# Reordering the side work of the paired MLP stage: when a tile is added and scaled, when the next pair's operands are turned, combined and split, and when the weight combinations are made

## The chip, the cores and the metric

The kernel runs on one core of one Trainium2 chip. The metric is device time in microseconds (us) of one execution; three runs of the kernel before gave 3091.52, 3093.77 and 3094.1 us, median 3093.77. The engines are named as in the profile: PE (TensorE, matrix products), DVE (VectorE), ACT (ScalarE), POOL (GpSimd), and SP, whose queue starts every DMA that is spoken of here.

## The reference, cut to what matters

`x` is 8192 tokens of 512 channels. It is normalised, sent through a state-space layer with an MLP behind it and, beside that, through a gated MLP on 4-bit quantised values; the results are added to `x`.

```
x   = L0_attn_x                                   # (2, 4096, 512)
xn  = layernorm(x)
a   = xn + ssm_scan(rmsnorm(xn, scale1))
h   = rmsnorm(a, scale2)
h   = gelu(h @ w1 + b1) @ w2 + b2                 # 512 -> 2048 -> 512
out = x + (a + h) + fp4_gated_mlp(xn)             # 512 -> 1408 -> 512
```

The change touches only the fourth and fifth line: the two products with `w1` and `w2` and what prepares their input.

## The kernel before, in words

The 8192 tokens are 64 tiles of 128. Up to about 1760 us the kernel does the quantised MLP, the convolution form of the scan and the first tiles' preparation. Then two stages follow.

**The block stage (about 1760 to 2099 us).** Sixteen tiles, four blocks of four, go through `mlp1(n)` (12 matmuls, one 128-wide slice of the hidden layer) and `mlp2(n)` (12 matmuls) for n = 0 to 63; PE runs `mlp1(n)`, `mlp2(n-2)`, `mlp1(n+1)`, and so on. Each float32 product is made as three products of a high and a low part. Between them, at fixed n, the other engines do side work. `mlp_steps` lists where the tiles of the next block are added (`tile_add`), scaled (`tile_root`) and split (`tile_low`, `tile_high`). `early_steps` lists the same for the first eight tiles of the next stage, at n = 44 to 57. `combine_steps` lists where 16 pieces of `w1` are combined for the next stage: ACT scales (`combine_scale`), POOL makes four sums (`combine_sums`, L2222 to L2227), ACT takes the high part (L1995), POOL the low part (`combine_low`, L2233, `wl`), and SP stores both.

**The paired stage (2099 to 3092 us).** Six pairs of blocks, 8 tiles (1024 tokens) each. `unit(c, u)`, u = 0 to 7, makes the first product by a seven-product scheme (`product`, L1203, 42 matmuls: k = 0 to 6) whose results DVE adds up (L1671, L1676, L1682, L1692, L1696) and ACT sends through gelu. `rest(c)` finishes the second product (`second(c, i, j)`, L1225, 12 matmuls for each i from 14 to 31). PE's order is fixed: in the rest it does i = 14, 15, 16, ... without anything between. For each i DVE copies the high part of the gelu's result (`second_part`, L1660, the CAST rows) and POOL subtracts to get the low part (`second_rest`, L2249). The buffers G, G2x hold three such i, so DVE may copy i when PE has finished i - 3, and PE needs copy and low part when it comes to i.

Side work in a unit, for the next pair's tile `o`: SP loads it, DVE does `tile_add` (L1542, L1546), ACT squares it, POOL adds bias and residual (`tile_z`, L2208, L2213), DVE does `tile_root` (L1552, ten instructions on one column, then L1558 over the tile), SP stores the sum (`store_sum`, L718) and the scaled tile (`store_normed`, L722, to `r_N`).

Side work in a rest, for the next pair: its tiles come back from `r_N` in four quarters (`quarters(c, i)`, L741, eight DMAs with 128-byte pieces). Quarter 1 overwrites the buffers of tile 7, so it waits until that tile's `store_normed` has landed (`d_ho`). Then for each quarter DVE transposes twice (`conv_turn`, L1612), makes four half-size sums in PSUM (`conv_sums`, L1628, L1629, L1631, L1633), ACT takes high parts (`conv_high`), DVE and POOL take low parts (`conv_low`, L1639/L1643 on DVE, L2239/L2242 on POOL). The sums use PSUM banks 0 to 3, which hold the second product's first half until `sum_out` (L1708) has read them. All engines run their queues in program order, so a wait of one instruction holds all behind it.

## Time and profile before

| | |
|---|---|
| median of 3 runs | 3093.77 us |
| the profiled execution, device time | 3093.77 us |
| its span, first to last instruction | 3092.0 us |
| PE busy | 2991.3 us (97%) |
| DVE busy | 2177.3 us (70%) |
| ACT, POOL busy | 1146.4 us (37%), 1519.8 us (49%) |
| mean granted PE clock | 0.998 |

PE is busy nearly all the time; the other engines matter only where they make it wait. The 12 matmuls of one i are issued in 2.72 us (the row of 24 that starts at 2218.18 is followed by the next i at 2223.76). A row's own duration is longer, since matmuls overlap.

### The profile page before, as it was taken

The numbers are of one execution on the slowest core, as the hardware profiler recorded it, in microseconds if no ns is written. First come the engines' busy times: TensorE is split into PE (matmuls) and PEld (weight loads), VectorE is DVE, ScalarE is ACT, GpSimd is POOL, SyncE is SP. The second block draws the span as 40 slices with busy tenths as digits, with TensorE's granted clock in tenths as the row PEclk, the third lists the DMA queues.
The fourth block names the chain that finished last, engine by engine and source line by source line (L and its number), as shares of the span: only waits on it lengthen the run. The fifth ranks groups of instructions, "written<-read, shape, count | busy, mean of one in ns | idle before, by whom it ended". The sixth has DMA issues, their size and how long they took to land.

```text
span 3092.0 us, 43985 instructions
## 1 busy us (share of the span) xinstructions
PE 2991.3 (97%) x14573; PEld 2417.7 (78%) x14573; DVE 2177.3 (70%) x4451; ACT 1146.4 (37%) x1934; POOL 1519.8 (49%) x1417
## 2 busy tenths in 40 slices
PE   5799999999999999999999899999999999999999
PEld 3678888888887777777777788788888888888887
DVE  7798898887877677777777676776665656565622
ACT  5445656644453343433433343222222222222220
POOL 7556666665555555554555235423444434353513
PEclk9999999999999999999999999999999999999999
DMA  4133343346766666666643458777777676768541
GB/s 126 48 86 93 118 118 107 97 133 180 191 175 171 162 168 163 154 162 172 166 120 99 126 134 203 170 178 205 203 179 205 174 214 168 206 165 218 150 127 48
DMA packets 965425, 469.89 MB, mean 152 GB/s; under 512 B 688080, under 2 KB 816336, under 8 KB 962640
## 3 DMA queue, kind: packets, MB, share of 16 engines
q1 hardware_dynamic: 965200, 467.08, 58.0%
q8 instruction: 118, 1.93, 0.3%
q14 instruction: 107, 0.88, 0.1%
HBM read 330.06 MB, written 136.87 MB: 151 GB/s over the span
## 4 chain that ended last, share of the span: by engine, by line
PE 66%; DVE 18%; issue 5%; POOL 5%; DMA 2%; ACT 2%; SPq 1%; DVEq 0%; POOLq 0%; ACTq 0%
PE bank L1225 16%; PE bank L1203 15%; PE bank L1029 14%; PE bank L1051 7%; PE bank L1152 4%; PE bank L1168 4%; DVE qs L1349 3%; POOL qa L2124 2%; DVE qa L1366 2%; PE bank L1092 2%; DVE qs L1360 2%; DVE qa L1322 2%; POOL qa L2118 1%; DVE qb L1374 1%; PE bank L999 1%
## 5 line engine op out<-in xcount | busy, mean ns | idle before, releaser
L1029 PE MATMUL bank<-XT,Wu 128*128 128x512 f32 (+1 forms) x2148 | 515.5, 389 | 16.1 <-DVE sg L1314 15.8
L1029 PE MATMUL bank<-XT,Wg 128*128 128x512 f32 (+1 forms) x2148 | 522.8, 392 | 7.3 <-DVE Wd L1381 7.3
L1051 PE MATMUL bank<-Wd,HT 128*128 128x512 f32 x2112 | 515.5, 393 | 6.6 <-POOL HT L2132 5.3
L1029 PEld LDWEIGHTS bank<-XT,Wu 128*128 128x128 f32 x2148 | 400.9, 190 | 106.7 <-issue 25.9
L2124 POOL TENSOR_TENSOR qa<-qb,qs 128x512 f32<-128x512 f32 (+2 forms) x277 | 308.5, 1114 | 342.3 <-DVE qb L1374 337.8
L1051 PEld LDWEIGHTS bank<-Wd,HT 128*128 128x128 f32 x2112 | 391.8, 188 | 106.2 <-issue 15.4
L1029 PEld LDWEIGHTS bank<-XT,Wg 128*128 128x128 f32 x2148 | 397.4, 189 | 95.9 <-DVE Wd L1381 9.4
L1225 PE MATMUL bank<-Wp,G 128*128 128x512 f32 x1536 | 388.4, 389 | 5.1 <-POOL G L2249 5.1
L1203 PE MATMUL bank<-HC,Wp 128*128 128x512 f32 x1440 | 361.7, 389 | 1.7 <-POOL WH L2242 1.7
L2132 POOL TENSOR_TENSOR HT<-qb,HT 128x512 fp32r<-128x512 f32 (+1 forms) x179 | 229.9, 1284 | 242.2 <-ACT HT L1817 242.0
L1225 PEld LDWEIGHTS bank<-Wp,G 128*128 128x128 f32 x1536 | 288.1, 188 | 66.1 <-POOL G L2249 6.3
L2118 POOL TENSOR_TENSOR qa<-qa,qs 128x512 f32<-128x512 f32 (+1 forms) x243 | 263.0, 1082 | 109.1 <-DVE qs L1354 109.1
L1203 PEld LDWEIGHTS bank<-HC,Wp 128*128 128x128 f32 x1440 | 270.2, 188 | 58.2 <-POOL WH L2242 2.1
L1817 ACT ACTIVATE HT<-qb 128x512 fp32r<-128x512 f32 (+1 forms) x179 | 112.2, 627 | 414.1 <-DVE qb L1328 414.0
L1366 DVE SCALAR_TENSOR_TENSOR qa<-qb,qa 128x512 f32<-128x512 f32 (+2 forms) x149 | 120.8, 811 | 140.7 <-ACT qb L1789 140.5
L2249 POOL TENSOR_TENSOR G<-gf,G 128x512 fp32r<-128x512 f32 x64 | 83.4, 1304 | 254.9 <-DVE G L1660 254.9
L1225 PE MATMUL bank<-Wp,G2x 128*128 128x512 f32 x768 | 198.1, 389 | 3.4 <-POOL G2x L2249 3.4
L1152 PE MATMUL bank<-hT,Wp 128*128 128x512 f32 x768 | 188.3, 395 | 8.1 <-DVE Wp L1537 5.4
L1168 PE MATMUL bank<-Wp,G 128*128 128x512 f32 x768 | 184.7, 390 | 4.4 <-DVE G L1588 3.2
L1824 ACT ACTIVATE sg<-bank 128x512 f32<-128x512 f32 (+1 forms) x179 | 105.5, 590 | 203.7 <-PE bank L1029 200.3
L1152 PEld LDWEIGHTS bank<-hT,Wp 128*128 128x128 f32 x768 | 146.4, 191 | 39.5 <-issue 5.8
L1168 PEld LDWEIGHTS bank<-Wp,G 128*128 128x128 f32 x768 | 144.0, 188 | 36.0 <-DVE G L1588 6.0
(199 smaller groups left out, 4543.4 us busy)
## 6 DMA issues: line engine op xcount, KB each, us to landing
Wp<-r_A SPq DMA_DIRECT2D x336, 256.0 KB, 3.5
px<-in_L_attn_x_dram SPq DMA_DIRECT2D x128, 256.0 KB, 3.3
xin<-in_L_attn_x_dram SPq DMA_DIRECT2D x128, 256.0 KB, 3.4
sT<-r_K SPq DMA_DIRECT2D x128, 256.0 KB, 4.2
r_Z<-xin SPq DMA_DIRECT2D x64, 256.0 KB, 2.4
r_U<-ub SPq DMA_DIRECT2D x16, 1024.0 KB, 6.7
sU<-r_U SPq DMA_DIRECT2D x32, 512.0 KB, 5.1
r_Y<-sY SPq DMA_DIRECT2D x16, 1024.0 KB, 5.6
```

The source lines that it names most:

```text
L1029: ins = e.matmul(bk[:, 0:n], W[wh][:, k, :], inputs(xh, w, k), start=(k == 0 and p_ == 0), stop=(k == KD - 1 and p_ == 2))
L1051: ins = e.matmul(DNB[t % 4][:], HT[hh][:, w % 2, a * P:(a + 1) * P], Wd[wh][:, f, :], start=(w == first(n) and p_ == 0), stop=(w == last(n ...
L1152: ins = e.matmul(bk[:], Wp[f][wh][:, 0, k * P:(k + 1) * P], hT[xh][b % 2][:, k, :], start=(k == 0 and p_ == 0), stop=(k == KD - 1 and p_ = ...
L1168: ins = e.matmul(ACC[j][:], G2[gh][:, n % 2, j * P:(j + 1) * P], Wp[f][wh][:, 1, :], start=(f == 0 and p_ == 0), stop=(f == 15 and p_ == 2))
L1203: ins = e.matmul(bank[bk][:], ring(q)[:, 256 * wh_ + P * kt:256 * wh_ + P * kt + P], combined(b, xh)[:, kt], start=(k in OPENS and kt == 0 ...
L1225: ins = e.matmul(bank[4 * half + j][:], (second_high(q), second_low(q))[gh][:, j * P:(j + 1) * P], Wp[f][wh_][:, 1, :], start=(f == 0 and ...
L1366: e.scalar_tensor_tensor(Aa, Bb, FLOOR, Aa, ALU.max, ALU.add).then_inc(s_t, 1)
L1817: e.activation(HT[0][:, w % 2, 0:n], qb[:, m % 2, 0:n], ACT.Copy).then_inc(s_hh, 1)
L1824: e.activation(sg[:, 0:n], GB[:, 0:n], ACT.Silu).then_inc(s_sg, 1)
L2118: e.tensor_tensor(blk(qa[:, m % 4, 0:n]), blk(job_in(m)), bc(qs[:, m % 4, 1, 0:n // 16], n // 16), ALU.mult).then_inc(s_pa, 1)
L2124: e.tensor_tensor(blk(qa[:, m % 4, 0:n]), blk(qb[:, m % 2, 0:n]), bc(qs[:, m % 4, 0, 0:n // 16], n // 16), ALU.mult).then_inc(s_ph, 1)
L2132: e.tensor_tensor(lo, qb[:, m % 2, 0:n], hi.bitcast(F32), ALU.subtract).then_inc(s_hl, 1)
```

## The change

Five things move; no instruction's work is changed.

1. `combine_steps`: the 16 combinations stand at n = 18, 20, ..., 48 instead of 12, 14, ..., 42.
2. In a unit, `tile_add` stands before the copy `second_part(c, 2u)` and L1682 (behind them before); `tile_root` stands before L1696 (behind it before); on ACT `tile_square` moves ahead of a gelu; on SP `store_sum` moves from k = 5 to k = 4.
3. In a rest, DVE's `conv_turn` stands at i = 17, 18, 24, 26 (before: 17, 21, 26, 29), `conv_sums` at 20, 21, 25, 28 (20, 23, 27, 30), `conv_low` at 22, 23, 27, 29 (22, 25, 28, 31), and the first four `sum_out` all at i = 19 (two at 19, two at 21). POOL's `conv_low` stands at 17, 20, 25, 27 (18, 22, 27, 30).
4. ACT's `conv_high` takes the first two parts of quarters 0 and 1 first; `high_done` counts accordingly.
5. SP issues `quarters(c+1, 2)` behind the loads of residuals 4 to 7.

```diff
 def combine_steps(n):
-    return [k for k in range(16) if 12 + 2 * k == n]
+    return [k for k in range(16) if 18 + 2 * k == n]
...
 sync: unit
-                    if k == 5 and more:
+                    if k == 4 and more:
                         store_sum(o)
 sync: rest
                 for i in range(4):
                     tile_result(c, i)
-                if more:
-                    quarters(c + 1, 2)
                 for i in range(4, 8):
                     residual_in(c, i)
                 if more:
+                    quarters(c + 1, 2)
                     quarters(c + 1, 3)
 vector: unit
                 e.tensor_tensor(u3[:], bank[6][:], u2[:], ALU.add).then_inc(s_add, 1)
+                if c + 1 < PAIRS:
+                    tile_add(o)
                 second_part(c, 2 * u if u < 7 else 14)
...
-                if c + 1 < PAIRS:
-                    tile_add(o)
...
                 e.tensor_tensor(gelued(0, 2 * u + 1), bank[6][:], u2[:], ALU.add).then_inc(s_add, 1)
+                if c + 1 < PAIRS:
+                    tile_root(o)
...
                 e.tensor_tensor(gelued(1, 2 * u), bank[7][:], u2[:], ALU.add).then_inc(s_add, 1)
-                if c + 1 < PAIRS:
-                    tile_root(o)
                 if u == 7:
                     second_part(c, 15)
 vector: rest
-                    if i in (19, 21):
-                        sum_out(c, i - 19)
-                        sum_out(c, i - 18)
-                    if i in (17, 21, 26, 29) and more:
-                        conv_turn(d, (17, 21, 26, 29).index(i))
...
+                    if i in (17, 18, 24, 26) and more:
+                        conv_turn(d, (17, 18, 24, 26).index(i))
+                    if i == 19:
+                        for j in range(4):
+                            sum_out(c, j)
...
```

**Place one: DVE, the end of a pair's unit 7** (first pair). L1682, L1692, L1696 add up products 4, 5 and 6; L1542 and L1546 are `tile_add`; L1552 to L1558 are `tile_root`; the last CAST is the copy for i = 15. Before:

```order
L1676 TENSOR_TENSOR u<-bank,u 128x512
L1660 CAST G2x<-GX 128x512
L1682 TENSOR_TENSOR G<-bank,u 128x512
L1542 TENSOR_SCALAR xl<-xl,mv,rst 128x512
L1546 TENSOR_TENSOR xl<-xl,yl 128x512
L1692 TENSOR_TENSOR gf<-bank,u 128x512
L1696 TENSOR_TENSOR G<-bank,u 128x512
L1552 TENSOR_SCALAR rs<-rs 128x1
...
L1558 TENSOR_SCALAR xl<-xl,rs 128x512
L1660 CAST G<-GX 128x512
```

The same place in the changed kernel, whose line numbers are 3 to 5 higher (L1695 is L1692, L1555 is L1552, L1561 is L1558, L1701 is L1696, L1663 is L1660):

```order
L1549 TENSOR_TENSOR xl<-xl,yl 128x512
L1663 CAST G2x<-GX 128x512
L1687 TENSOR_TENSOR G<-bank,u 128x512
L1695 TENSOR_TENSOR gf<-bank,u 128x512
L1555 TENSOR_SCALAR rs<-rs 128x1
...
L1561 TENSOR_SCALAR xl<-xl,rs 128x512
L1701 TENSOR_TENSOR G<-bank,u 128x512
L1663 CAST G<-GX 128x512
```

The scaling now lies between the additions of products 5 and 6, and the copy for i = 15 follows the last addition directly.

**Place two: DVE, the rest, i = 17 to 21.** L1612 are the transposes of `conv_turn`, the L1660 rows the copies, L1708 `sum_out`, L1628 to L1633 `conv_sums`. Before, from the transposes of quarter 0:

```order
L1612 STREAM_TRANSPOSE xl<-yl 128x512
L1660 CAST G<-GX 128x512 x2
L1708 TENSOR_TENSOR zq<-bank,zq 128x512 x2
L1660 CAST G2x<-GX 128x512
L1628 TENSOR_TENSOR bank<-xl,st 128x256
L1629 TENSOR_TENSOR bank<-xl 128x256
L1631 TENSOR_TENSOR bank<-xl,bank 128x256
L1633 TENSOR_TENSOR bank<-st,bank 128x256
L1660 CAST G<-GX 128x512
L1708 TENSOR_TENSOR gf<-bank,gf 128x512 x2
L1612 STREAM_TRANSPOSE yl<-xl 128x512
L1612 STREAM_TRANSPOSE xl<-yl 128x512
```

In the changed kernel (L1615 transposes, L1663 copies, L1711 `sum_out`, L1631 to L1636 `conv_sums`), the copy for i = 18 is the first CAST:

```order
L1663 CAST G<-GX 128x512
L1615 STREAM_TRANSPOSE yl<-xl 128x512
L1615 STREAM_TRANSPOSE xl<-yl 128x512
L1663 CAST G<-GX 128x512
L1711 TENSOR_TENSOR zq<-bank,zq 128x512 x2
L1711 TENSOR_TENSOR gf<-bank,gf 128x512 x2
L1663 CAST G2x<-GX 128x512
L1631 TENSOR_TENSOR bank<-xl,st 128x256
L1632 TENSOR_TENSOR bank<-xl 128x256
L1634 TENSOR_TENSOR bank<-xl,bank 128x256
L1636 TENSOR_TENSOR bank<-st,bank 128x256
L1663 CAST G<-GX 128x512
```

The transposes of quarter 1 moved ahead of the copy for i = 19, the four `sum_out` ahead of the copy for i = 20.

**Place three: POOL, the end of the combinations in the block stage.** L2222 to L2227 are the sums, L2233 is `combine_low`, L2208 and L2213 are `tile_z`. Before:

```order
L2222 TENSOR_TENSOR wt<-wt 128x128
L2223 TENSOR_TENSOR wt<-wt 128x128
L2225 TENSOR_TENSOR wt<-wt 128x128
L2227 TENSOR_TENSOR wt<-wt 128x128
L2233 TENSOR_TENSOR wl<-wt,wh 128x1024
L2208 TENSOR_TENSOR zl<-zl,b2r 128x512
L2213 TENSOR_TENSOR yl<-zl,xl 128x512
```

In the changed kernel (L2225 to L2230 the sums, L2236 `combine_low`, L2211 and L2216 `tile_z`):

```order
L2211 TENSOR_TENSOR zl<-zl,b2r 128x512
L2216 TENSOR_TENSOR yl<-zl,xl 128x512
L2225 TENSOR_TENSOR wt<-wt 128x128
L2226 TENSOR_TENSOR wt<-wt 128x128
L2228 TENSOR_TENSOR wt<-wt 128x128
L2230 TENSOR_TENSOR wt<-wt 128x128
L2236 TENSOR_TENSOR wl<-wt,wh 128x1024
L2211 TENSOR_TENSOR zl<-zl,b2r 128x512
```

The first row that writes `zl` is the first of the next stage's tiles: before, all combinations lay ahead of these tiles; now the last three lie among them.

## Rows read from the trace of the kernel before

**Rows 1.** PE's waits, paired stage: engine line <- releaser: us, times, longest.

```profile
PE bank L1225 <- POOL G L2249: 5.1, 3, 1.7
PE bank L1225 <- POOL G2x L2249: 3.4, 2, 1.7
```

**Rows 2.** PE's waits from 1820 to 2025 us, block stage.

```profile
PE bank L1168 <- DVE G L1588: 3.2, 2, 1.8
...
PE bank L1168 <- DVE zx L1599: 1.2, 2, 0.7
```

**Rows 3.** Timeline of PE, first rest: start us, us, what, [idle before <- releaser].

```profile
2213.61 2.88 PE L1225 MATMUL bank<-Wp,G2x 128*128 128x512 f32 x12
2218.18 5.74 PE L1225 MATMUL bank<-Wp,G 128*128 128x512 f32 x24 [1.69 <-POOL G L2249]
2223.76 2.88 PE L1225 MATMUL bank<-Wp,G2x 128*128 128x512 f32 x12
```

**Rows 4.** Timeline of DVE and POOL, end of unit 7.

```profile
2211.09 0.69 DVE L1692 TENSOR_TENSOR gf<-bank,u 128x512 f32<-128x512 f32 x1 [0.17 <-PE bank L1203]
2213.13 0.69 DVE L1696 TENSOR_TENSOR G<-bank,u 128x512 f32<-128x512 f32 x1 [1.35 <-PE bank L1203]
...
2213.74 0.14 DVE L1552 TENSOR_SCALAR rs<-rs 128x1 f32<-128x1 f32 x1
...
2216.26 0.42 DVE L1660 CAST G<-GX 128x512 fp32r<-128x512 f32 x1
...
2216.76 1.38 POOL L2249 TENSOR_TENSOR G<-GX,G 128x512 fp32r<-128x512 f32 x1 [3.60 <-DVE G L1660]
2216.93 1.48 DVE L1660 CAST G2x<-gf 128x512 fp32r<-128x512 f32 x1
```

**Rows 5.** Timeline of SP's queue, first rest, and one row of the third.

```profile
2216.37 0.32 SPq L722 DMA_DIRECT2D r_N<-xl  x1
...
2218.81 2.60 SPq L741 DMA_DIRECT2D xl<-r_N  x4
2221.46 2.67 SPq L741 DMA_DIRECT2D yl<-r_N  x4
...
2546.75 0.32 SPq L722 DMA_DIRECT2D r_N<-xl  x1
2550.28 1.24 SPq L741 DMA_DIRECT2D xl<-r_N  x2
```

**Rows 6.** DMA issues, 2210 to 2218.5 us, then 2218.5 to 2224.5: median us to landing.

```profile
Wp<-r_A SPq DMA_DIRECT2D x4, 256.0 KB, 4.7
...
r_N<-xl SPq DMA_DIRECT2D x1, 256.0 KB, 2.3
...
yl<-r_N SPq DMA_DIRECT2D x4, 64.0 KB, 2.4
```

**Rows 7.** Timeline of DVE and POOL, first rest, i = 20 to 23.

```profile
2226.75 0.43 DVE L1660 CAST G2x<-GX 128x512 fp32r<-128x512 f32 x1 [0.74 <-PE bank L1225]
...
2229.65 0.42 DVE L1660 CAST G<-GX 128x512 fp32r<-128x512 f32 x1
...
2229.99 1.28 DVE L1708 TENSOR_TENSOR gf<-bank,gf 128x512 f32<-128x512 f32 x2
...
2231.18 0.70 DVE L1612 STREAM_TRANSPOSE yl<-xl 128x512 f32<-128x512 f32 x1
...
2232.56 0.38 DVE L1660 CAST G<-GX 128x512 fp32r<-128x512 f32 x1
...
2234.27 1.29 POOL L2239 TENSOR_TENSOR HC<-yl,HC 128x512 fp32r<-128x512 f32 x1
...
2235.52 0.92 POOL L2242 TENSOR_TENSOR WH<-xl,WH 128x256 fp32r<-128x256 f32 x1
```

**Rows 8.** Timeline of POOL and DVE around n = 44.

```profile
1981.57 2.50 POOL L2233 TENSOR_TENSOR wl<-wt,wh 128x1024 fp32r<-128x1024 f32 x1 [1.17 <-ACT wh L1995]
1981.88 2.73 DVE L1588 TENSOR_TENSOR G<-gf,G 128x512 fp32r<-128x512 f32 x1
```

More of the change, by code:

```diff
@@ L482, in high_done @@
         def high_done(c, i, x):
-            return 20 * c + 5 * i + x + 1
+            order = [(a, b) for a in range(4) for b in range(5)]
+            if c:
+                order = ([(a, b) for a in (0, 1) for b in (0, 1)] + [(a, b) for a in (0, 1) for b in (2, 3, 4)]
+                         + order[10:])
+            return 20 * c + order.index((i, x)) + 1
         def combined(m, h):
@@ L1714, in rest @@
                     second_part(c, i)
-                    if i in (19, 21):
-                        sum_out(c, i - 19)
-                        sum_out(c, i - 18)
-                    if i in (17, 21, 26, 29) and more:
-                        conv_turn(d, (17, 21, 26, 29).index(i))
-                    if i in (20, 23, 27, 30) and more:
-                        conv_sums(d, (20, 23, 27, 30).index(i))
-                    if i in (22, 25, 28, 31) and more:
-                        conv_low(d, (22, 25, 28, 31).index(i))
+                    if i in (17, 18, 24, 26) and more:
[3 more added lines that the diff above has]
+                            sum_out(c, j)
+                    if i in (20, 21, 25, 28) and more:
+                        conv_sums(d, (20, 21, 25, 28).index(i))
+                    if i in (22, 23, 27, 29) and more:
+                        conv_low(d, (22, 23, 27, 29).index(i))
                 for j in range(4, 8):
@@ L2043, in unit @@
                 e.activation(gelued(0, 2 * u), bank[4][:], ACT.Gelu, bias=vec[:, 2 * u:2 * u + 1]).then_inc(s_gc, 1)
+                if c + 1 < PAIRS:
+                    tile_square(OLD + 8 * (c + 1) + u)
                 for n, (half, f) in enumerate(((1, 2 * u + 1), (0, 2 * u + 1), (1, 2 * u))):
@@ L2046, in unit @@
                     e.activation(gelued(half, f), gelued(half, f), ACT.Gelu, bias=vec[:, f:f + 1]).then_inc(s_gc, 1)
-                    if n == 0 and c + 1 < PAIRS:
-                        tile_square(OLD + 8 * (c + 1) + u)
             def rest(c):
                 if c + 1 < PAIRS:
-                    for i in range(4):
-                        for x in range(5):
-                            conv_high(c + 1, i, x)
+                    for i, x in ([(a, b) for a in (0, 1) for b in (0, 1)] + [(a, b) for a in (0, 1) for b in (2, 3, 4)]
+                                 + [(a, b) for a in (2, 3) for b in range(5)]):
+                        conv_high(c + 1, i, x)
             for m in range(NJ + 4):
@@ L2263, in rest @@
                     second_rest(c, i)
-                    if i in (18, 22, 27, 30) and c + 1 < PAIRS:
-                        conv_low(c + 1, (18, 22, 27, 30).index(i))
+                    if i in (17, 20, 25, 27) and c + 1 < PAIRS:
+                        conv_low(c + 1, (17, 20, 25, 27).index(i))
             for m in range(NJ + 3):
```

## The prediction

> **What bounds the kernel now.** I read the busy shares first (PE 97%), then PE's waits by stage, because with PE this full only its waits can be won. From its start at 2099 us the paired stage has 8.5 us of waits for the low part that POOL makes, five of them [rows 1]; from 1820 to 2025 us PE waits 4.4 us for DVE [rows 2]. The earlier stages are not touched. Parts one to three speak of the five waits; of the rest only half of the 1.2 us for L1599 lies where the change frees anything. So all that can be won is some 10 us, 0.3% of 3092.
>
> The five waits are one wait five times. In the timeline of the first rest PE starts i = 14 at 2213.61. Twelve matmuls take 2.72 us (24 of them end with the next start: (2223.76 - 2218.18) / 2 = 2.79, of which 0.07 is a slower re-entry), so i = 15 could start at 2216.33; it starts at 2218.18, 1.85 us late [rows 3]. DVE's timeline says why: L1696 starts at 2213.13, the scaling of the tile fills 2213.74 to 2216.26, only then comes the copy for i = 15, POOL's low part follows at 2216.76, and PE goes 1.92 us after the copy's start [rows 4]. All that follows is arithmetic on this ledger; every time is of the first rest.
>
> **Part one, the scaling moved ahead of L1696.** L1692 starts at 2211.09 and its successor 0.61 us later, as L1696's does [rows 4]. The scaling takes 2216.26 - 2213.74 = 2.52 us, so L1696 starts at 2211.70 + 2.52 = 2214.22, the copy at 2214.83, and PE at 2214.83 + 1.92 = 2216.75. The wait shrinks from 1.85 to 0.42 us: 1.43 us won, 7.2 us in five rests. POOL is idle there before the copy (3.60 us in its row), so nothing lengthens the scaling. L1696 is 1.1 us later; what waits for it is the fourth bank of i = 14 at 2213.61 + 2.04 = 2215.65, after its end at 2214.91. In units 0 to 6 its readers are the next unit's fifth product, several us away: nothing. `tile_add` now starts after L1676, some 5 us earlier than before; its load is issued a unit ahead: nothing. The sooner store of the sum and the moved square cost nothing either: PE waits for neither, and both only come before the scaling that needs them.
>
> **Part two, the transposes of quarter 1 at i = 18.** This is the step that can take the gain back. DVE now waits, with the copy for i = 19 behind it, until quarter 1 has landed. Before, they stood at 2231.18 [rows 7], long after. Quarter 1 starts when the scaled tile 7 has landed in `r_N`: stored at 2216.37, first quarter DMA at 2218.81, the eighth 4.7 us later, and landed 2.4 us after that: 2225.9 [rows 5, 6]. In the third rest the same step took 3.53 us instead of 2.44 [rows 5]; the five are 2.44, 3.24, 3.53, 3.46 and 2.66 us, mean 3.07. These differences are not the store's own time: it took 2.3 us to land in the first rest, when the four ring loads issued just before it took 4.7 [rows 6], so the queue was still draining loads. In the changed kernel the store is issued at 2214.33, 2.04 us earlier, but behind the same loads. At best all 2.04 us are won, at worst none, as the loads decide. I take 1.2: SP gets to quarter 0 and the loads behind it about 1 us sooner, since tile 6 too is stored sooner. Then quarter 1 has landed, on the average of five rests, at 2225.9 + 0.63 - 1.2 = 2225.3.
>
> The Trainium skill, "DMA: Bandwidth & Descriptors", section on queues, rings and completion order, says that each of the 16 DMA engines takes a ring's descriptors in order, while completion of whole DMAs is not in order of issue. By it the store stays behind the loads. The 4.7 and 2.3 us agree with a queue that drains; no run here shows one DMA engine by itself.
>
> From the landing the ledger goes on. Two transposes and the step to the copy take 2232.56 - 2231.18 = 1.38 us [rows 7]: the copy for i = 19 starts at 2226.7, PE can start i = 19 at 2228.6. PE wants it at 2216.75 + 4 x 2.72 + 0.1 = 2227.7. A new wait of 0.9 us. (With the landing at 2223.9 it would be none; at 2226.5, 2.1.)
>
> **Part three, what follows at i = 19 to 22.** Four `sum_out` in a row, at (2231.18 - 2229.99) / 2 = 0.60 us each [rows 7], behind 0.34 us for the copy, put the copy for i = 20 at 2229.5: PE could have it at 2231.4, wants it at 2231.3, no wait worth counting. POOL then does the low part of 20 and the two low parts of quarter 1, which stood at i = 22: 1.29 + 0.92 us [rows 7], and only then that of 21. That ends 0.5 + 1.3 + 2.2 + 1.3 = 5.3 us after the copy for 20, at 2234.8; PE wants i = 21 at 2234.1: 0.7 us. DVE's second `conv_sums` takes 2.9 us like the first (2229.65 - 2226.75) [rows 7], and leaves i = 22 late by 0.1 to 0.2. From i = 23 DVE is ahead again: quarters 2 and 3 land about 5 us before PE needs what is made of them. The conversions end earlier than before, but PE has no wait at a next pair's start that could go (the five of [rows 1] are all in the rests), so that wins nothing.
>
> Sum of a rest: 0.42 + 0.9 + 0.7 + 0.15 and 0.07 to 0.1 us of re-entry at each of three: 2.4 us, against 1.85 + 0.11 before: +0.4 us, five times: +2 us. Bounds: quarter 1 early and no collision, 5 x (0.42 - 1.96) = -7.7 us; landings as before, 5 x (3.7 - 1.96) = +8.7 us.
>
> A rule speaks against part three. The Trainium skill, "SBUF — State Buffer", section on the shared port pair, says that GpSimd and a VectorE copy (or an operation with two SBUF inputs) lock each other out for a whole instruction. The trace agrees: a copy of 0.42 us took 1.48 where a POOL operation of 1.38 us had started before it [rows 4]. The 2.9 us of `conv_sums` hold one such stop; by the rule the second one, now beside POOL's extra pair, could hold a second of 1.3 us.
>
> **Part four, the combinations 6 steps later.** At n = 18 to 42 the same work stands as before, so I leave those waits as they are. At 12 to 17 POOL and ACT are freed; the only wait near is half of the 1.2 us for L1599 [rows 2]: at most 0.6 us won. At 43 to 49 three combinations join the additions and scalings of four tiles. What such a meeting costs is in the rows: L1588 took 2.73 us instead of 0.69 beside L2233's 2.50 [rows 8], and PE's two waits for L1588 are 3.2 us [rows 2]. L1599 at n = 49, for which PE waits 0.7 us already [rows 2], gets the last combination just before it. Bounds -0.6 and +6 us (three meetings of 2 us); I take +1.5, one such wait (1.6), as DVE runs ahead of PE in most of that stretch.
>
> **Sum.** The profiled execution took 3093.8 us, which is also the median (span 3092.0). 3093.8 + 2 + 1.5 = 3097.3, so 3097 us. This kernel's measurement tells 0.2%, 6 us, from no change.
>
> **Rivals.**
> - *The waits simply go* (faster). Quarter 1 lands by 2223.9, POOL and DVE don't collide, and part four is neutral: 3093.8 - 7.7 = 3086 us. For it: the store is issued 2.04 us sooner, SP is less behind. Against: the quarter-1 step took up to 3.53 us before, in a queue full of loads.
> - *The landing decides* (slower). The ring loads hold the store, quarter 1 lands when it did, DVE stands at i = 18 with the copy for 19 behind it: +8.7, with part four +10: 3104 us. It decides from a landing 0.6 us later than I take. For it: in four of five rests the wait for the landing was over 2.6 us.
> - *The combinations among the early tiles* (slower). Rest as forecast, three meetings instead of one: +2 + 6 = 3102 us. Against it: no wait at 44 to 48 now, so there is slack to eat first.
>
> **How the numbers follow.** My forecast, within 0.2% (3087.6 to 3100): 0.45. The waits simply go: 0.22. The landing decides 0.23, the combinations 0.10: slower 0.33. The likeliest is the forecast, 3097 us. The range: 3086 holds nearly all of the faster case, whose end is about the most that can be won; 3107 covers both slower cases and part of their sum. So 3086 to 3107; the forecast's own range is 3089 to 3100.
>
> **What would show it.** Part one: the rests' wait at i = 15 at 0.4 us, the copy for i = 15 right behind the last addition. Part two: DVE idle before the third transpose, released by a DMA, and PE waiting for POOL's low part at i = 19. Part three: PE waiting at i = 21, POOL's `conv_low` pair just before. Part four: new waits of PE for L1588's successor between 1987 and 2020 us and a longer one for L1599's. It would be wrong if the rests have no wait at all, if the scaling between the additions made a unit's product wait, or if waits appear at i = 24 or later.

## The result and the profile after

| | before | changed |
|---|---|---|
| median (4 runs each, same chip) | 3093.93 us | 3112.88 us |
| lowest to highest | 3091.52 to 3094.47 | 3110.65 to 3115.39 |
| ratio, with 95% interval | | 1.0062 [1.005, 1.0075] |
| the profiled execution, device time | 3093.77 us | 3109.46 us |
| its span | 3092.0 us | 3107.7 us |

The changed kernel is slower by 19 us. The forecast was 3097 us with a range of 3086 to 3107, so the time lies 6 us beyond the upper end, and it isn't within 0.2% of the kernel before either. Over all 21 executions on record the changed kernel took 3109.46 to 3116.33 us. The profiled one is the lowest of them, 3.4 us below the median of the four, so its trace accounts for 15.7 us of the 19. One execution of the kernel before, beside the first four experiments, took 6119.76 us at a mean granted clock of 0.543; no comparison uses it.

The page of the changed kernel, busy time and share of the span by engine, then PE's waits in the paired stage (from 2098 us; engine, line, releaser: us in total, times, longest):

```profile
PE 2998.3 (96%) x14573; PEld 2417.2 (78%) x14573; DVE 2148.6 (69%) x4451; ACT 1142.6 (37%) x1934; POOL 1519.4 (49%) x1417
```

```profile
PE bank L1228 <- POOL G L2252: 8.3, 10, 2.4
PE bank L1228 <- POOL G2x L2252: 3.5, 5, 1.5
PE bank L1206 <- DVE GX L1687: 2.6, 1, 2.6
PE bank L1206 <- POOL WH L2245: 1.8, 1, 1.8
```

The five waits for the low part [rows 1] have become fifteen, 11.8 us where 8.5 stood, and there is a sixteenth for DVE, which did not exist. PE's busy time rose by 7 us with the same 14573 matmuls, for two reasons. After a wait the next two matmuls come later than the idle time says (at i = 15 it is 0.27 us of idleness, a start 0.43 us late and another 0.11 us for the matmul behind it), so each new wait costs about 0.27 us more than it shows; and some matmuls ran at the lower clock, of which more below.

By stage, from the starts of PE's matmuls: up to n = 2 of the block stage -1.0 us (1735.2 before, 1734.2 after; over all kernels profiled here this point lies between 1734.0 and 1736.1, so that is scatter), from there to the first matmul of the paired stage 370.5 instead of 364.0 us, and the paired stage 1002.9 instead of 992.7 us. So two places lost 6.5 and 10.2 us.

**The paired stage.** Timeline of the first rest in the changed kernel, PE, DVE, POOL and SP's queue put together (start us, us, what, [idle before <- releaser]):

```profile
2221.97 2.88 PE L1228 MATMUL bank<-Wp,G2x 128*128 128x512 f32 x12
2222.57 0.68 DVE L1701 TENSOR_TENSOR G<-bank,u 128x512 f32<-128x512 f32 x1
2222.68 0.32 SPq L726 DMA_DIRECT2D r_N<-xl  x1
2223.17 0.42 DVE L1663 CAST G<-GX 128x512 fp32r<-128x512 f32 x1
2225.12 5.73 PE L1228 MATMUL bank<-Wp,G 128*128 128x512 f32 x24 [0.27 <-POOL G L2252]
2226.87 2.60 SPq L745 DMA_DIRECT2D xl<-r_N  x4
2229.51 2.67 SPq L745 DMA_DIRECT2D yl<-r_N  x4
2235.52 0.71 DVE L1615 STREAM_TRANSPOSE yl<-xl 128x512 f32<-128x512 f32 x1 [6.21 <-DMA yl<-r_N]
2236.91 0.38 DVE L1663 CAST G<-GX 128x512 fp32r<-128x512 f32 x1
2238.69 3.06 PE L1228 MATMUL bank<-Wp,G 128*128 128x512 f32 x12 [2.40 <-POOL G L2252]
...
2241.46 1.48 POOL L2242 TENSOR_TENSOR HC<-yl,HC 128x512 fp32r<-128x512 f32 x1
2242.90 0.92 POOL L2245 TENSOR_TENSOR WH<-xl,WH 128x256 fp32r<-128x256 f32 x1
2245.29 5.82 PE L1228 MATMUL bank<-Wp,G 128*128 128x512 f32 x24 [0.72 <-POOL G L2252]
```

This is the ledger of the forecast with real numbers in it. The copy for i = 15 follows the last addition at once (L1701 2222.57, CAST 2223.17) and PE starts i = 15 at 2225.12, 0.43 us late instead of 1.85 [rows 3]. Then DVE stands for 6.21 us in front of quarter 1; the copy for i = 19 comes at 2236.91 and PE sits idle for 2.4 us there. At i = 21 POOL has the pair L2242, L2245 ahead of PE's low part, and PE is 0.9 us late. ("Late" is the matmul's start against the 227 ns at which matmuls follow each other; it is 0.16 us more than the idle time in brackets.) Over the five rests i = 15 is late by 0.43 to 0.44 us; i = 19 by 2.56, 0.77, 1.69, 0.72 and 1.97 (mean 1.54); i = 21 by 0.87 to 0.90.

The landing that sets i = 19 came, counted from the start of i = 14, after 13.53, 11.77, 12.66, 11.67 and 12.99 us, mean 12.5; before it was 12.32 to 13.47, mean 13.0. The store of tile 7 was issued 2.05 us sooner. The DMA issues of the changed kernel around it (2221 to 2226.5 us) tell where that went; the last number is the median us to landing:

```profile
Wp<-r_A SPq DMA_DIRECT2D x1, 256.0 KB, 4.6
r_N<-xl SPq DMA_DIRECT2D x1, 256.0 KB, 4.0
```

The same store needed 2.3 us to land before [rows 6]. It was issued 2.05 us sooner and took 1.7 us longer. Over the five rests it took 3.7 to 5.0 us (mean 4.3) where it took 2.3 to 3.4 before (mean 2.9), so 0.7 of the 2.05 us were won. In the first rest the last of the eight quarter DMAs also landed 3.95 us after its issue instead of 2.44, so that this landing came 1.2 us later than before, and the mean gain at the landing is 0.44 us. That the loads ahead of the store hold it is what the rows suggest; no run takes the loads away. e10 below moves the same store the other way: issued 1.27 us later, it took 2.0 to 2.7 us (mean 2.2) and landed only 0.5 us later.

The sixteenth wait is in the first unit of the first pair. Timeline of SP's queue, DVE and PE there, changed kernel:

```profile
2107.85 0.34 SPq L699 DMA_DIRECT2D xl<-in_L_attn_x_dram  x1
2108.24 2.54 SPq L705 DMA_DIRECT2D yl<-r_Y  x2
2114.03 0.69 DVE L1549 TENSOR_TENSOR xl<-xl,yl 128x512 f32<-128x512 f32 x1 [2.08 <-DMA yl<-r_Y]
2114.97 0.69 DVE L1687 TENSOR_TENSOR GX<-bank,u 128x512 f32<-128x512 f32 x1
2115.71 1.67 PE L1206 MATMUL bank<-WH,Wp 128*128 128x512 f32 x6 [2.56 <-DVE GX L1687]
```

For every later unit the tile's load is issued a unit ahead. This one is issued in the unit that uses it: `tile_add` now meets it before it has landed, and the addition of product 4 (L1687), for which PE waits, stands behind.

**The block stage.** PE's waits in the changed kernel from 1985 to 2030 us:

```profile
PE bank L1171 <- DVE zx L1602: 5.8, 1, 5.8
PE bank L1155 <- ACT gf L1980: 2.2, 2, 1.9
```

Before, the same window has 0.75 us for L1599, L1602's predecessor, and at its left edge the end of a wait of 1.8 us for L1588 at 1984.7, which the changed kernel has at 1979.0 (1.5 us), outside. The timeline of POOL, DVE and PE in the changed kernel shows how 0.75 became 5.8:

```profile
1993.58 1.99 DVE L1293 SCALAR_TENSOR_TENSOR rs<-rs 128x1 f32<-128x1 f32 x1
...
1998.85 0.63 ACT L1945 ACTIVATE yl<-xl 128x512 f32<-128x512 f32 x1 [6.83 <-DVE xl L1549]
...
2006.16 0.49 DVE L1561 TENSOR_SCALAR xl<-xl,rs 128x512 f32<-128x512 f32 x1
...
2007.09 2.87 POOL L2236 TENSOR_TENSOR wl<-wt,wh 128x1024 fp32r<-128x1024 f32 x1 [1.17 <-ACT wh L1998]
2007.63 2.62 DVE L1545 TENSOR_SCALAR xl<-xl,mv,rst 128x512 f32<-128x512 f32 x1
2010.29 1.66 DVE L1549 TENSOR_TENSOR xl<-xl,yl 128x512 f32<-128x512 f32 x1
...
2017.74 2.34 POOL L2236 TENSOR_TENSOR wl<-wt,wh 128x1024 fp32r<-128x1024 f32 x1 [1.17 <-ACT wh L1998]
2017.79 2.57 DVE L1561 TENSOR_SCALAR xl<-xl,rs 128x512 f32<-128x512 f32 x1
...
2021.34 2.48 DVE L1602 TENSOR_TENSOR zx<-bank,zx 128x512 f32<-128x512 f32 x4
...
2022.17 4.52 PE L1171 MATMUL bank<-Wp,G 128*128 128x512 f32 x12 [5.82 <-DVE zx L1602]
```

The last combinations now lie among `tile_add` and `tile_root` of the next stage's tiles. L1561 takes 0.49 us by itself and 2.57 beside POOL's L2236; L1545 takes 2.62 instead of 0.54; L1549 1.66 instead of 0.69. These three are 2.08 + 2.08 + 0.97 = 5.1 us, and the wait grew by 5.1, but that is not yet the whole account. The same stretch before starts and ends with these rows:

```profile
2002.03 0.43 DVE L1586 CAST G<-gf 128x512 fp32r<-128x512 f32 x1 [1.37 <-ACT gf L1977]
...
2017.54 2.48 DVE L1599 TENSOR_TENSOR zx<-bank,zx 128x512 f32<-128x512 f32 x4
```

From the copy to the result's additions that is 15.51 us; in the changed kernel, from the same copy at 2000.18 to L1602 at 2021.34, it is 21.16, so 5.65 more. The three stops make 5.13 of it, the one-column instructions of the two scalings 1.49, as they now also meet POOL's four sums, and two stops by `tile_z` that stood there before are 0.99 shorter. The idle 1.36 us of DVE ahead of a copy are no slack: ACT's square waits for the `tile_add`, the gelu stands behind the square, and the copy needs the gelu.

The wait of 1.9 us for ACT at 2000.3 comes in the main in the same way, one tile earlier: L1293, on one column, takes 1.99 us instead of 0.16 beside a L2236 of 2.84 us that started at 1992.70, the `tile_add` behind it is late, and ACT's square waits 6.83 us for it. So far this is arithmetic on rows; e9 below shortens such POOL operations and sees what goes. The Trainium skill, "SBUF — State Buffer", section "SBUF: two separate sides", says that a VectorE operation in a mode that uses two ports and a GpSimd operation exclude each other for the whole of one instruction, whichever started first. The trace agrees: POOL's operation ends at 2020.08, and DVE's, which started beside it, 0.28 us later.

And a long wait costs twice. The windows of 2022.0 to 2025.5 us, changed kernel, and of 2022 to 2026 us, before (start:end, us, busy PE (x), PEld (x), DVE (x), ACT (x), POOL (x), granted PE clock, DMA share, GB/s):

```profile
2022.00:2025.50 3.50, 3.33 (x8) 2.68 (x9) 3.47 (x6) 0.00 (x0) 1.28 (x1) 0.51 0.82 177
```

```profile
2022.00:2026.00 4.00, 4.00 (x20) 3.30 (x19) 2.50 (x7) 1.99 (x4) 1.29 (x1) 1.00 0.93 250
```

After the 5.8 us of idleness the granted clock is 0.51, that is 1.2 GHz: 8 matmuls stand 427 ns apart instead of 227. The row of twelve takes 4.52 us instead of 3.01 at the same step before, after a wait of 0.75: 1.5 us more; after the 1.94 us wait at 2000.3 it is 1.4. In sum the stretch from n = 44 to the paired stage lost 7.3 us of waits (5.1 + 1.9 + 0.3) and some 3.5 of clock and slower starts behind the waits, 11 us. That the stage lost only 6.5 comes from an old wait at its start: 5.42 us before a first matmul at 1764.2, followed by matmuls at the lower clock, became 2.99 at full clock. In the profiles of kernels that leave this stage as it was, this wait lies anywhere from 2.9 to 5.4 us, so I don't count it to the change. The wait for L1588 at 1984 us scatters in the same way: 1.8 to 3.6 us in the eight profiles that have the combinations at 12.

### The profile page after: what moved, and what is told of

Same layout as the page of the kernel before. It is cut to its first block, busy times and chain, and to the rows that moved or that the text cites. A ratio compares the mean times of both kernels' runs of the same rounds, so it can differ in the third digit from the quotient of the medians.

```text
span 3107.7 us, 43985 instructions
## 1 busy us (share of the span) xinstructions
PE 2998.3 (96%) x14573; PEld 2417.2 (78%) x14573; DVE 2148.6 (69%) x4451; ACT 1142.6 (37%) x1934; POOL 1519.4 (49%) x1417
## 4 chain that ended last, share of the span: by engine, by line
PE 62%; DVE 18%; issue 6%; POOL 5%; DMA 4%; ACT 2%; SPq 2%; DVEq 0%; ACTq 0%; POOLq 0%
PE bank L1032 14%; PE bank L1206 14%; PE bank L1228 14%; PE bank L1054 7%; PE bank L1155 4%; PE bank L1171 3%; DVE qs L1352 3%; POOL qa L2127 2%; DVE qa L1369 2%; PE bank L1095 2%; DVE qs L1363 2%; DVE qa L1325 2%; POOL qa L2121 1%; DVE qb L1377 1%; PE bank L1002 1%
```

## The experiments

All are edits of the kernel before or of the changed one, 5 to 11 executions each, against the kernel before. Its median was 3094.15 us beside the first four, 3093.96 beside the next four, 3092.88 beside the last four. "Stage" numbers are from the profile of each run: block stage 364.0 and paired stage 992.7 us for the kernel before.

| run | median us | ratio [95%] | block, paired stage |
|---|---|---|---|
| e1_comb18: before, combinations at 18 + 2k | 3101.5 | 1.0027 [1.0017, 1.0038] | 370.5, 992.7 |
| e2_nocomb: changed, combinations back at 12 | 3105.2 | 1.0035 [1.0021, 1.0048] | 364.3, 1005.3 |
| e3_unit: before, only the unit's reordering | 3090.2 | 0.9991 [0.9982, 0.9999] | 365.5, 988.6 |
| e4_rest: before, only the rest's reordering | 3103.15 | 1.0032 [1.002, 1.0045] | 363.6, 1004.0 |
| e5_turn19: e2, quarter 1 turned at i = 19 | 3102.36 | 1.0031 [1.002, 1.0043] | 363.1, 1001.8 |
| e6_turn19_pool22: e5, POOL's pair at i = 22 | 3103.12 | 1.0036 [1.0022, 1.005] | 362.7, 1000.5 |
| e7_comb16: before, combinations at 16 + 2k | 3100.78 | 1.0026 [1.0015, 1.0036] | 372.7, 992.8 |
| e8_comb6: before, combinations at 6 + 2k | 3096.72 | 1.0008 [0.9999, 1.0017] | 366.3, 992.7 |
| e9_comb18_narrow: e1, last low parts short | 3096.28 | 1.0011 [1.0003, 1.002] | 366.7, 992.9 |
| e10_copyfirst: before, copy 15 before the scaling | 3085.76 | 0.9977 [0.9968, 0.9986] | 362.4, 985.6 |
| e11_unit_g0: e3 but for the first unit | 3087.11 | 0.9979 [0.9971, 0.9988] | 363.6, 986.4 |
| e12_copyfirst_comb10: e10, combinations at 10 + 2k | 3087.77 | 0.9985 [0.9976, 0.9994] | 365.2, 985.6 |

The paired stage of the kernel before repeats within 0.3 us (992.7 to 992.9 in five profiles); the block stage, with the combinations where they were, lies between 362.4 and 365.5. So a paired stage in which no landing is waited for can be read to a fraction of a microsecond, the block stage only to one or two. Where DVE waits for the landing, the paired stage scatters too: the changed kernel and e2 have the same code there and 1002.9 and 1005.3 us. Of these 2.4 us, 1.5 are the first unit's (e2's wait of 2.47 us was followed by matmuls at the lower clock), the rest other landings.

### Which part costs: e1_comb18, e2_nocomb

e1, on the kernel before:

```diff
-    return [k for k in range(16) if 12 + 2 * k == n]
+    return [k for k in range(16) if 18 + 2 * k == n]
```

> The kernel before with the combinations alone at n = 18 to 48. Theory A (the combinations among the early tiles carry the loss): slower by 9 to 13 us, with PE's waits of about 2 us near n = 46 and 6 us for the result's additions at n = 49 of the changed kernel's profile here too, and the five rests with their 1.7 us as before. Theory B (the landing of quarter 1 carries it): slower by 0 to 3 us.

e2, on the changed kernel, is the same line turned back.

> The changed kernel with the combinations back at n = 12 to 42. Theory A: slower than before by 4 to 9 us: five rests with waits of 0.3, 0.6 to 2.4 and 0.7 us, and the 2.6 us wait in the first pair's unit 0. Theory B: nearly all of the 19 us stays, over 14 us.

e1 costs 7 to 8 us, less than the 9 to 13 expected, and all of it in the block stage. Its waits from 1985 to 2030 us are much like those of the changed kernel, though the one for ACT stands at 2015.3 instead of 2000.3:

```profile
PE bank L1168 <- DVE zx L1599: 5.8, 1, 5.8
PE bank L1152 <- ACT gf L1977: 1.7, 1, 1.7
```

e2 costs 11 us, all of it in the paired stage. That lies between the two theories, 4 to 9 and over 14, and nearer to the first. The two halves add up: 7.4 + 11.1 = 18.5 us, against 19 for the whole.

### Inside the paired stage: e3_unit, e4_rest

e3 takes over the moves of `tile_add`, `tile_root`, `tile_square` and `store_sum` and leaves the rest as it was; e4 takes over the moves in the rest (`conv_turn`, `conv_sums`, `sum_out`, `conv_low`, `conv_high`, the quarters' order) and leaves the unit. The core of e3, then of e4:

```diff
+                if c + 1 < PAIRS:
+                    tile_root(o)
                 e.wait_ge(s_p, 7 * g + 7)
...
-                if c + 1 < PAIRS:
-                    tile_root(o)
```

```diff
-                    if i in (17, 21, 26, 29) and more:
-                        conv_turn(d, (17, 21, 26, 29).index(i))
+                    if i in (17, 18, 24, 26) and more:
+                        conv_turn(d, (17, 18, 24, 26).index(i))
```

> The kernel before with the unit's reordering alone (addition and scaling earlier, square, store of the sum). The rests of before keep their order, with quarter 1 turned at i = 21. If the ledger's part one holds: each rest waits 0.3 to 0.4 us instead of 1.7, 7 us won, less 2.6 us for the first pair's unit 0, where the addition waits for a load that has just been issued: faster by 3 to 5 us. Rival: the earlier scaling in itself makes waits in units or rests: not faster.

> The kernel before with the rest's reordering alone (turns, sums, sum_out, low parts, quarters). If the wait at i = 19 comes from the landing of quarter 1 and the loss at i = 21 from POOL's order: each rest keeps its 1.7 us and adds waits at i = 19 and 21 of about 1 to 2 us in sum, slower by 5 to 12 us. Rival: the rests' new waits are there only since the scaling moved and took the 1.7 us of slack away: under 3 us slower.

Both as expected. PE's waits of e3 in the paired stage, then of e4:

```profile
PE bank L1203 <- DVE GX L1684: 2.4, 1, 2.4
...
PE bank L1225 <- POOL G L2249: 0.8, 3, 0.3
PE bank L1225 <- POOL G2x L2249: 0.5, 2, 0.3
```

```profile
PE bank L1228 <- POOL G L2252: 9.0, 7, 2.1
PE bank L1228 <- POOL G2x L2252: 6.0, 5, 1.7
```

e3 has the forecast's 0.43 us at each i = 15 (idle time of up to 0.3 us and the re-entry), and the 2.4 us of the first unit as its only new wait: the paired stage is 4.1 us shorter. e4 keeps the five waits of 1.85 us and adds new ones at i = 19 (2.29, 0.53, 1.36, 0.17 and 0 us late) and i = 21 (0.87 in four rests; in the first, matmuls at the lower clock take 1.5 us in its place): 11.3 us longer. The parts don't add up: 4.1 won and 11.3 lost would make +7.2 us for e2's stage, which has +12.6. The difference is mostly at i = 19: PE comes 1.4 us sooner out of i = 15, and the landing comes only 0.5 us sooner (12.7 us after the start of i = 14 on the average, 13.2 in e4). Most of what is won at i = 15 is given back four steps later: e2 is late there by 2.46, 1.47, 1.72, 1.55 and 1.34 us, 0.84 a rest more than e4. One subtraction gives all these: in e2 and in the changed kernel the lateness at i = 19 is the landing less 10.97 us, in e4 the landing less 12.39, within 0.05 us in the fourteen rests where this is above zero; in the fifteenth PE isn't late.

### Where the landing is waited for: e5_turn19, e6_turn19_pool22

```diff
-                    if i in (17, 18, 24, 26) and more:
-                        conv_turn(d, (17, 18, 24, 26).index(i))
+                    if i in (17, 19, 24, 26) and more:
+                        conv_turn(d, (17, 19, 24, 26).index(i))
```

> As e2 (all of the change but the combinations), with the transposes of quarter 1 at i = 19 instead of 18, so that the copy for i = 19 stands ahead of the wait for the landing. Theory L (the landing, with a copy queued behind it, makes the wait at i = 19): the waits of 1.3 to 2.5 us at i = 19 go, at i = 20 less than 0.8 us takes their place, since the copy behind the transposes is due 2.7 us later; the 0.9 us at i = 21 stay: 5 to 8 us less than e2. Theory C (DVE simply has too much to do from i = 18 to 22): the time moves by less than 2 us, as the wait only moves on.

One step of i is 2.7 us and the lateness at i = 19 was about 1.7 us, so one step should have been enough. It wasn't: a miss. The median went down by 3 us, and of the 3.5 us in the profile 1.9 are the first unit's, where e2 had matmuls at the lower clock. The five rests together are only 1.5 us shorter, as theory C said. Timeline of the first rest of e5:

```profile
2231.29 0.41 DVE L1663 CAST G2x<-GX 128x512 fp32r<-128x512 f32 x1
2233.20 3.04 PE L1228 MATMUL bank<-Wp,G2x 128*128 128x512 f32 x12 [2.20 <-POOL G2x L2252]
2236.94 3.30 PE L1228 MATMUL bank<-Wp,G 128*128 128x512 f32 x13 [0.70 <-POOL G L2252]
```

The wait went to i = 20 (2.36, 1.38, 0.88, 0.44 and 2.14 us late). At i = 19 the four `sum_out`, 2.4 us together, also stand between the transposes and the copy for i = 20, so the step of 2.7 us that was gained was nearly used up by them. The landing still decides: in all five rests the lateness at i = 20 is the landing less 11.2 us, where that at i = 19 was the landing less 11.0. In the kernel before only two of them stand there, and the transposes come two steps later still.

e6 moves POOL's pair of quarter 1 (L2242, L2245) from i = 20 to i = 22, on e5:

```diff
-                    if i in (17, 20, 25, 27) and c + 1 < PAIRS:
-                        conv_low(c + 1, (17, 20, 25, 27).index(i))
+                    if i in (17, 22, 25, 27) and c + 1 < PAIRS:
+                        conv_low(c + 1, (17, 22, 25, 27).index(i))
```

> As e5, with POOL's low parts of quarter 1 at i = 22 instead of 20. If the 0.9 us wait at i = 21 is POOL's order (second_rest(21) behind two operations of 2.2 us), it goes: 4 to 5 us less than e5, about the time of e3 (3090). If it is DVE's copy that is late, the wait stays.

A miss. The waits of 0.87 us at i = 21 are gone (0.14 us is left in one rest), which shows them to be POOL's order, but four rests are 0.69 to 0.73 us late at i = 23 instead, and the first rest lost by the clock what it won. The same wait, followed by another clock, in e6:

```profile
2233.65 4.61 PE L1228 MATMUL bank<-Wp,G2x 128*128 128x512 f32 x12 [2.00 <-POOL G2x L2252]
```

In e5 the twelve matmuls after 2.20 us of idleness took 3.04 us, in e6 after 2.00 us they took 4.61. The paired stage went from 1001.8 to 1000.5 us, and the medians don't tell the two kernels apart.

### Where the combinations may stand: e7_comb16, e8_comb6, e9_comb18_narrow

e7 and e8 are e1's line with 16 and with 6 in place of 18.

> The kernel before with the combinations at n = 16 to 46. If the 6 us wait for the result's additions comes from the last low part (2.3 us on POOL) standing at n = 49, with the scaling of an early tile locked out beside it: that wait falls back to about 1 us, while the wait of 2 us near n = 47 stays: slower than before by 2 to 4 us (e1: 8). Rival (each step of delay costs alike, 1.3 us a step): slower by 5 us.

> The kernel before with the combinations at n = 6 to 36, that is earlier. If it is their meeting with the tiles added and scaled at n = 33 to 43 that makes PE's waits of 1.6, 2.8 (and 7 matmuls at half clock) and 1.9 us there, these go or halve: faster than before by 3 to 7 us. Rival (these waits come from the tiles' own round trip through DRAM, and the early combinations meet the weights' split at n = 6 to 13): within 2 us or slower.

e7 is a miss. I had expected that two steps less would cure most of it; it costs the same 7 us as e1. The wait for L1599 is 3.1 us instead of 5.8, but L1588's at 1985 us is 3.7 where e1 has 2.3. As kernels with the combinations at 12 have 1.8 to 3.6 there, this one profile doesn't show that the place made it. e8 is a miss too: 3 to 7 us faster was expected, and its median is 2.8 us higher (the interval of its ratio just includes 1). The wait for L1588 at 1984 us is gone, as in no other kernel but e12, but those of 1.5 and 2.5 us at 1930 and 1969 us stay, and new ones came at 1793 to 1827 us, where the combinations now start. None of the three places tried here (6, 16, 18) is better than 12; the cost depends on which pairs of instructions meet.

e9 is e1 with the low parts of the last three combinations narrowed from eight columns of blocks to one, so that POOL's operation lasts 0.64 to 0.94 us. It leaves out seven eighths of these low parts:

```diff
-                e.tensor_tensor(wl[k % 2][:], wt[:, k % 2], wh[:].bitcast(F32), ALU.subtract).then_inc(s_wal, 1)
+                n = 8 if k < 13 else 1
+                e.tensor_tensor(wl[k % 2][:, 0:n], wt[:, k % 2, 0:n], wh[:, 0:n].bitcast(F32), ALU.subtract
+                                ).then_inc(s_wal, 1)
```

> As e1 (the combinations alone at n = 18 to 48), with POOL's low part of the last three (n = 45, 47, 49) made over an eighth of its columns, 0.3 us instead of 2.3; the rest of those low parts is left out, so the third stage reads old values in their place. All waits, loads, stores and ACT's and POOL's other operations stay. Theory A1 (POOL's long operation locks DVE's scaling and additions out): the 6 us wait for the result's additions falls to 1 to 2 us, e1's 8 us fall to 3 or less. Theory A2 (ACT's and SP's added work and the DMA traffic do it): the waits stay, 3 us less than e1 at most.

DVE's last scaling in e1, beside the last low part, and in e9, where that low part starts only at 2018.23:

```profile
2019.73 2.34 POOL L2233 TENSOR_TENSOR wl<-wt,wh 128x1024 fp32r<-128x1024 f32 x1 [1.17 <-ACT wh L1995]
2019.77 2.58 DVE L1558 TENSOR_SCALAR xl<-xl,rs 128x512 f32<-128x512 f32 x1
```

```profile
2017.01 0.49 DVE L1558 TENSOR_SCALAR xl<-xl,rs 128x512 f32<-128x512 f32 x1
```

Against the kernel before e9 costs 3.4 us where e1 costs 7.4. More than half of the cost goes with the length of three POOL operations. The forecast of 1 to 2 us for the wait missed: PE still waits 3.2 us for L1599 there, 2.5 more than before. The rows tell where 2.0 of them are: the one-column instructions of the last two scalings take 5.07 and 2.80 us, where the kernel before has 3.87 and 2.11, beside POOL's four sums, which e9 keeps, and L1542 is 0.14 longer. No run takes the sums away, so this part is read and not tested. The size of this wait also hangs on the one at 1984 us: with the combinations at 12, PE waits 1.8 to 2.4 us there and 0.5 to 0.75 at L1599 in three profiles, and 2.2 to 3.6, each time with matmuls at the lower clock behind it, and then nothing in the other five. e12, whose combinations are over by then, has no wait at 1984 us and 2.3 at L1599.

### What can be won: e10_copyfirst, e11_unit_g0, e12_copyfirst_comb10

If the scaling only has to get out of the way of the copy for i = 15, the simplest edit is to exchange the two:

```diff
-                if c + 1 < PAIRS:
-                    tile_root(o)
                 if u == 7:
                     second_part(c, 15)
+                if c + 1 < PAIRS:
+                    tile_root(o)
```

> The kernel before with one exchange: in unit 7 the copy for i = 15 stands ahead of the tile's scaling. All else is as before. The five waits of 1.7 us go whole (5 x 1.96 us); quarter 1 starts some 0.3 us later, which nothing waits for, as its transposes stand at i = 21: faster by 9 to 10 us, 3084. Rival (the waits were what gave DVE and POOL time to follow in the rest): new waits in the rests, gain under 5 us.

This has the lowest median of the study, 3085.76 us, 7 us less than the kernel before, ratio 0.9977 [0.9968, 0.9986]; e11, at 0.9979, can't be told from it. Timeline of its first rest:

```profile
2212.76 0.42 DVE L1660 CAST G<-GX 128x512 fp32r<-128x512 f32 x1
...
2215.35 2.88 PE L1225 MATMUL bank<-Wp,G 128*128 128x512 f32 x12
...
2216.55 0.42 DVE L1660 CAST G<-gf 128x512 fp32r<-128x512 f32 x1
...
2218.52 3.03 PE L1225 MATMUL bank<-Wp,G 128*128 128x512 f32 x12 [0.28 <-POOL G L2249]
```

i = 15 starts without a wait. The wait has moved to i = 16, whose copy now stands behind the scaling, and is 0.44 us there: 1.4 us won per rest, 7.1 in the paired stage, where 9 to 10 were expected: the wait didn't go whole. The store of tile 7 is issued 1.27 us later, quarter 1 lands at 13.4 to 14.5 us after the start of i = 14 (12.3 to 13.5 before), and the transposes of quarter 1 stay at i = 21, where nobody meets it.

e11 is e3 with `tile_add` and its square left in the old place for the first unit alone (`if c + 1 < PAIRS and g:` at the new place, `if g == 0:` at the old).

> As e3 (the unit's reordering alone), but in the first pair's unit 0 the addition and the square keep their old places. If the 2.6 us wait there is the load issued just before the stage, with L1682 queued behind the addition: it goes, 3 us less than e3, 3087. Otherwise the time is e3's.

As expected: against e3 the wait of 2.4 us is missing and the paired stage is 2.2 us shorter; the one other difference is a wait of 0.36 us for L1684 in the second pair. That shows the cause of the sixteenth wait. The medians agree with it, but by their intervals the two kernels just overlap.

e12 adds to e10 the combinations at 10 + 2k, to free the step at 1984 us.

> As e10, with the combinations at n = 10 to 40. They then end ahead of n = 44, where PE waits 1.9 to 3.9 us for L1588 beside the last low part, and start behind most of the weights' split (which made waits at n = 7 to 13 with the combinations at 6): 1 to 3 us less than e10. Rival: they meet the split at 10 to 13 as well: not less.

The wait at 1984 us went and one of 2.3 us came at 2017; the median is 2 us above e10's, within what two such kernels differ by. No gain: the rival held.

## Why the prediction was wrong, step by step

- **Part one, the wait at i = 15: right.** Forecast 0.42 us late, measured 0.43 to 0.44 in all five rests and in e3. The same step said of `tile_add` "its load is issued a unit ahead: nothing". That failed for the first unit of the first pair, the one whose load is issued in its own unit: a term put at nothing that cost 2.9 us (a start 2.7 us late and the slower starts behind it), shown by e11, which takes it away. The other units cost nothing, as said.
- **Part two, the landing: mis-sized.** I took 1.2 us of the store's 2.04 as won; the trace shows 0.44 (mean landing 13.0 to 12.5 us after i = 14's start), since the store took 4.3 us instead of 2.9 on the average, and in the first rest the last DMA of quarter 1 another 1.5. So i = 19 was late by 1.54 us on the average, not 0.9, and the landing was 0.8 us later than I took it, past the 0.6 us from which, in the prediction's own words, "the landing decides". That rival priced the rests at +8.7 us; they cost 7.4, read rest by rest. The row that could have told it stood in [rows 6]: the loads issued just before the store took 4.7 us.
- **Part three, POOL's order: nearly right.** 0.7 us forecast at i = 21, 0.88 measured; the lateness at i = 22 didn't come. A second stop of 1.3 us in the second `conv_sums`, which the rule cited in the prediction made possible, didn't come: L1631 and L1632 take 0.97 and 1.50 us there, and in the kernel before the same two rows (L1628 and L1629, at 2235.76 and 2236.64) take 0.97 and 1.51.
- **A rest as a whole** was to cost 0.4 us more than before. It cost 7.4 / 5 = 1.5. Of the 1.1 us between, 0.64 is the landing and 0.18 POOL's order; about 0.3 are slower starts behind the waits, more of them than my sum had, less the 0.15 for i = 22. The lower clock has no part in it: no rest of the changed kernel has a matmul at it (the first rests of e4 and e6 and the last of e5 do).
- **Part four, the combinations: this is the step that failed, by its size.** I took +1.5 us, "one such wait", from bounds of -0.6 and +6. Alone it costs 7 to 8 us (e1), beyond my upper bound. The mechanism, POOL's low part stopping DVE, was the right one. The bound of three meetings of 2 us was the better estimate, for the reason I gave against it didn't hold: that PE has no wait at n = 44 to 48 doesn't make DVE free there. The first stop already made PE wait for 1.9 us at 2000.3, and those behind it add up until PE waits for the result at n = 49. e9 shows more than half of the cost to hang on the length of three POOL operations; the rest I read from the rows as the sums beside one-column instructions, untested. What also lacked is the clock: two of the waits are followed by 7 or 8 matmuls at 1.2 GHz, 1.4 and 1.5 us more.
- **The sum.** +2 and +1.5 were forecast; the paired stage made 10.2 to 11 and the block stage 6.5 to 8. In the changed kernel's profile, which lies 12.2 us over the forecast, the combinations are 5.0 us over their term, the five rests 5.4 over theirs, the first unit 2.9, and 1.0 was won ahead of both stages by scatter; the 3.4 us to the median I can't place. Of the rivals, the truth is a sum of two that I priced apart: the landing (8.7 us in the rests) and the combinations among the early tiles (6). 3093.8 + 8.7 + 6 would have been 3108.5; the range took in only part of that sum.

What would have shown it in advance was named well: DVE idle before the third transpose, waits at i = 19 and 21, a longer wait for L1599's successor. That no wait appears for L1588's successor between 1987 and 2020 us, but one for ACT's gelu (1.9 us at 2000), was not foreseen: ACT's square stands behind DVE's `tile_add`, so a stop on DVE reaches PE through ACT's queue too.

Open: the 2.5 us by which e9's wait for L1599 exceeds the old one, as far as it isn't the sums; why e2 and the changed kernel have different landings with the same code; and the scatter of the waits at 1764 and 1984 us. The new order of ACT's `conv_high`, of quarter 2 and of the other `conv_turn` and `conv_sums` was only ever changed together (e4), and the four `sum_out` were not moved away from i = 19.

## What to carry to other kernels

Price a moved side task by what stands behind it in its queue and by whether the thing it waits for really comes sooner: a store that is moved up behind queued loads may land little sooner (0.7 of 2.05 us here), and a gain made ahead of such a landing is given back there. If the bottleneck waits for one copy, first try to move just that copy up (one exchange, -7 us here), before reordering what lies around it. When a loop's side work is moved, look at its first pass by itself, because its loads may not have the lead that the others have; and when long POOL operations are moved among short DVE ones, count every meeting as a full stop, the ones with the many short instructions too, as stops add up until somebody waits.

## What the runs showed of the hardware

- The lower clock after short waits. PE at a granted clock of 0.50 to 0.51 for 6 to 13 matmuls followed idle times of 1.94, 2.00 (e6), 2.6 (before, 1961.9; not in e3, 1959.9) and 5.8 us, but not those of 1.84 us (2104.7), 2.20 (e5, 2233.2), 2.40 (2238.7) and 2.99 us (1760.8). Here it adds 1.4 to 1.6 us to a wait of 2 us, or nothing.
- One instruction, two lengths: DVE's f32 scaling of 128x512 takes 0.49 us, and 2.57 us beside a POOL operation of 2.34. Operations on a single column are held too: L1293 took 1.99 us instead of 0.16 beside a POOL operation of 2.84.
- The 256 KB store of tile 7, by its time of issue after the start of i = 14, five rests each: issued at 0.7 us it lands after 3.7 to 5.0 us (changed kernel), at 2.8 after 2.3 to 3.4 (before), at 4.0 after 2.0 to 2.7 (e10). The landings, at 5.0, 5.7 and 6.2 us, move by less than half of what the issue moves.
